# Splitting the second attention layer's score tile into two halves of heads, half a slot apart

## The chip, the cores and the metric

One Trainium2 chip, one of its cores. The metric is the device time of one launch, in microseconds (us). The work runs on five engines that each take their own instructions in order and meet at semaphores: TensorE (PE in the profile, with its weight loads as PEld), VectorE (DVE), ScalarE (ACT), GpSimd (POOL) and SyncE (SP, which here only issues transfers).

## The reference, cut to what matters

Two gated layers over 64 sequences of 128 tokens with 256 features. Each layer is cross attention with 16 heads of 16 features, then a feed-forward part (a mixture of 64 experts in layer 0, a quantised one in layer 1).

```python
x = x + jnp.tanh(g_xattn[0]) * _L0_xattn_ref(_layernorm(x), ctx_1024, ctx_1024, ...)
x = x + jnp.tanh(g_ffn[0]) * _L0_ffn_ref(_layernorm(x), ...)
x = x + jnp.tanh(g_xattn[1]) * _L1_xattn_ref(_layernorm(x), ctx_1024, ctx_1024, mask_1x1xSxS2_ik0, ...)
x = x + jnp.tanh(g_ffn[1]) * _L1_ffn_ref(_layernorm(x), ...)
# _L1_xattn_ref, per sequence and head:
scores = jnp.einsum('bhqd,bhkd->bhqk', query, key_h) * scale
scores = jnp.where(mask == 0, jnp.float32(-1000000000.0), scores)
attn = jax.nn.softmax(scores, axis=-1)
x = jnp.einsum('bhqk,bhkd->bhqd', attn, value)
```

The change touches only the third line, the attention of layer 1.

## The kernel before

The attention of a layer is a software pipeline. One sequence is a tile; a slot handles up to eight tiles at different ages at once. In the code `f`, `m`, `k`, `o`, `w`, `v`, `u` are the tiles that are 0, 1, 2, 3, 4, 5 and 6 slots old, `g` is the next one. Each engine has a written-out order of steps for a slot (`body` in `attention_pe`, `attention_act`, `attention_dve`), and a loop repeats it over the slots. Nothing is planned at run time: an engine that waits holds up all that stands behind the wait.

The score tile `tiles` is four PSUM banks wide: 16 heads of 128 by 128 scores, float32, 2048 columns on 128 partitions. A layer-1 tile uses it twice:

- `scores(m)` (L442): TensorE writes the mask bias into all four banks (`masks(0)`, L426, 16 matmuls of 32x32 in bf16), then adds query times key. The 16 features of a head lie in one of four groups of 32 rows of the array, so that matmuls of four row groups can run side by side.
- `maximum(m)` (L940): VectorE takes the row maxima of all four banks into `mt`. `maxima_t` (L473) transposes `mt`, and `shifted(m)` (L952) adds the maxima to the queries, giving `qm`.
- `scores_t(k)` (L459): one slot later, the mask bias again and then the transposed scores, shifted by the maxima, in the same four banks; `exponent(k)` (L699): ScalarE takes the exponential of all four banks into `pt`.
- `values(o)` (L487, 32-column blocks of the array), `copy_ov` (L781), `heads_to_tokens` (L568), `head_sums` and `head_norm` (L1044, L1053), `tokens_to_heads` (L578), `copy_at` (L790), `output(w)` (L557), `residual(w)` (L964), `second_stats(w)` (L972) finish a tile. `project_qk(f)` (L527) and `transposes(g)` (L507) begin one.

There is one set of four banks, so scores and transposed scores take turns in it. `mask_keys(f)` (L734) on ScalarE makes the two masked copies of the keys from the block that SyncE has loaded (`load_keys_values`, L1225 and L1227). GpSimd does `inverse_roots` (L2091), `experts_sum` (L2118) and `add_bias` (L2102) for a slot. The order on TensorE in a slot of layer 1 is:

```python
scores(m); values(o); project_qk(f); transposes(g); scores_t(k)
heads_to_tokens(o); output(w); tokens_to_heads(o); maxima_t(m)
```

Layer 0 runs the same helpers with other masks and another order; in it TensorE goes from block to block without a wait.

## Time and profile before

| | |
|---|---|
| median of 3 runs | 1837.52 us (1836.88 to 1838.45) |
| the profiled execution | 1842.04 us, its span 1840.3 us |
| busy over the span | PE 1720.2 us (93%), DVE 1382.6 (75%), ACT 1169.1 (64%), POOL 668.5 (36%) |
| granted TensorE clock, mean | 0.983 |
| chain that ended last | PE 72%, DVE 17%, ACT 8% |
| largest single lines of that chain | DVE `mt` L940 8%, PE `tiles` L459 8%, PE `tiles` L442 8%, PE `bank` L527 7%, ACT `pt` L699 6% |

The busy share is an average over four stages. Layer 1's attention lies between about 1135 and 1630 us of the span. In a timeline row the first number is the start and the second the time that the group covers; ends of matmuls are modelled, so that differences of starts are the safer reading.

### The profile page before, as it was taken

How to read it: one execution, taken by the hardware profiler on the slowest of the kernel's cores; microseconds unless marked ns; L12 is line 12 of the kernel's file. 1: busy time of each engine (PE TensorE's matmuls, PEld its weight loads, DVE VectorE, ACT ScalarE, POOL GpSimd, SP SyncE). 2: the span in 40 equal slices, each digit the busy share in tenths (PEclk: the TensorE clock that was granted, in tenths of full speed). 3: DMA queues.
4: the chain of work that ended last, by engine and by line, in shares of the span. 5: the costliest groups of instructions: out<-in, count | busy, mean ns of one | idle time of the engine just before them, and what ended most of it. 6: DMA issues, size and time to landing. Idle time of an engine off the chain costs nothing.

```text
span 1840.3 us, 54611 instructions
## 1 busy us (share of the span) xinstructions
PE 1720.2 (93%) x20134; PEld 1343.9 (73%) x20144; DVE 1382.6 (75%) x4582; ACT 1169.1 (64%) x2411; POOL 668.5 (36%) x750
## 2 busy tenths in 40 slices
PE   5999999999999799999999998999999999968845
PEld 4888888888887688888888886677777777733334
DVE  4899999999998546655555544788888888759988
ACT  3777777777777233333323334788888888858875
POOL 1111111111111147777777774222222222211157
PEclk9999999999999899999999998999999999989989
DMA  3233333333334569888988885233332333203274
GB/s 104 83 95 95 95 98 107 98 96 101 98 95 153 173 187 233 220 223 206 223 216 217 216 178 154 83 96 93 89 88 88 89 94 95 69 35 138 103 279 178
DMA packets 231350, 247.64 MB, mean 135 GB/s; under 512 B 29680, under 2 KB 207216, under 8 KB 228912
## 3 DMA queue, kind: packets, MB, share of 16 engines
q1 hardware_dynamic: 206272, 205.54, 34.8%
q0 software_dynamic: 24816, 38.62, 11.6%
q8 instruction: 163, 2.67, 0.6%
q14 instruction: 99, 0.81, 0.1%
HBM read 142.40 MB, written 101.66 MB: 133 GB/s over the span
## 4 chain that ended last, share of the span: by engine, by line
PE 72%; DVE 17%; ACT 8%; issue 1%; SPq 1%; POOL 0%; DMA 0%; POOLq 0%; DVEq 0%; ACTq 0%
DVE mt L940 8%; PE tiles L459 8%; PE tiles L442 8%; PE bank L527 7%; ACT pt L699 6%; PE bank L403 6%; PE tiles L1464 6%; PE bank L383 6%; PE bank L487 4%; PE bank L557 3%; PE tiles L426 3%; PE bank L1478 3%; PE bank L540 3%; PE bank L413 3%; DVE hmax L1852 3%; PE tiles L1446 2%
## 5 line engine op out<-in xcount | busy, mean ns | idle before, releaser
L2091 POOL TENSOR_TENSOR rstd<-var,minus_half 128x2 f32<-128x2 f32 x140 | 97.9, 700 | 650.8 <-DVE var L1020 634.8
L940 DVE TENSOR_REDUCE mt<-tiles 128x16 f32<-128x2048 f32 x128 | 293.5, 2293 | 54.2 <-PE tiles L442 54.1
L699 ACT ACTIVATE pt<-tiles 128x2048 f32<-128x2048 f32 x128 | 240.7, 1880 | 48.1 <-PE tiles L459 48.1
L1639 POOL DMA_INDIRECT accumulator<-ye,tid x128 | 208.5, 1629 | 84.6 <-DVE ye L1583 54.3
L1583 DVE TENSOR_SCALAR ye<-bank,xr 128x256 f32<-128x256 f32 x128 | 56.1, 480 | 154.6 <-PE bank L1478 154.6
L2102 POOL TENSOR_TENSOR res<-res,bias 128x256 f32<-128x256 f32 x128 | 92.9, 725 | 205.8 <-ACT xn L758 203.1
L1624 POOL DMA_INDIRECT xr<-token_rows,tid x128 | 136.9, 1070 | 72.6 <-issue 35.1
L527 PE MATMUL bank<-xt,w_q 128*128 128x128 f32 x1024 | 155.2, 285 | 1.4 <-ACT xt L707 1.4
L459 PE MATMUL tiles<-qm,qkp 32*128 32x128 f32 x4096 | 151.1, 284 | 2.6 <-DVE mt L940 2.6
L442 PE MATMUL tiles<-qkp 32*128 32x256 f32 x2048 | 151.2, 409 | 1.8 <-ACT qkp L721 1.6
L459 PEld LDWEIGHTS tiles<-qm,qkp 32*128 32x128 f32 x4096 | 126.7, 187 | 28.4 <-issue 24.5
L527 PEld LDWEIGHTS bank<-xt,w_q 128*128 128x128 f32 x1024 | 131.9, 195 | 15.6 <-issue 13.6
L487 PE MATMUL bank<-pt,vx 128*32 128x128 f32 x4096 | 140.1, 278 | 1.6 <-ACT at L790 1.0
L487 PEld LDWEIGHTS bank<-pt,vx 128*32 128x32 f32 x4096 | 105.2, 110 | 44.5 <-issue 41.1
L557 PE MATMUL bank<-w_o,at 128*128 128x256 f32 x512 | 133.1, 383 | 1.7 <-ACT at L790 1.7
L952 DVE SCALAR_TENSOR_TENSOR qm<-bank,keep,qkp 128x256 f32<-128x256 f32 x256 | 111.1, 476 | 15.7 <-PE bank L473 15.6
L442 PEld LDWEIGHTS tiles<-qkp 32*128 32x128 f32 x2048 | 87.8, 186 | 40.8 <-issue 27.5
L719 ACT ACTIVATE qkp<-bank,qb 128x128 f32<-128x128 f32 x256 | 88.7, 372 | 36.3 <-PE bank L527 36.2
L675 ACT ACTIVATE res<-bank 128x256 f32<-128x256 f32 x64 | 24.5, 383 | 135.5 <-PE bank L403 135.5
L721 ACT ACTIVATE qkp<-bank,kb,keep 128x128 f32<-128x128 f32 x256 | 106.1, 483 | 0.0
L734 ACT ACTIVATE qkp<-cxax,kb,keep 128x128 f32<-128x128 f32 x256 | 105.4, 485 | 0.0
L557 PEld LDWEIGHTS bank<-w_o,at 128*128 128x128 f32 x512 | 88.0, 192 | 9.5 <-ACT at L790 2.9
(247 smaller groups left out, 4079.9 us busy)
## 6 DMA issues: line engine op xcount, KB each, us to landing
keys_values<-res SPq DMA_DIRECT2D x64, 256.0 KB, 2.9
cxax<-keys_values SPq DMA_DIRECT2D x128, 128.0 KB, 2.5
cxax<-accumulator SPq DMA_DIRECT2D x128, 128.0 KB, 2.2
hidden_away<-h_ring SPq DMA_DIRECT2D x8, 1536.0 KB, 5.0
token_rows<-pay SPq DMA_DIRECT2D x64, 160.0 KB, 1.8
pt<-in_expert_up SPq DMA_DIRECT2D x36, 256.0 KB, 3.5
cxax<-in_ctx SPq DMA_DIRECT2D x64, 128.0 KB, 2.2
res<-in_x SPq DMA_DIRECT2D x64, 128.0 KB, 2.3
```

Source lines behind the costliest of these rows:

```text
L383: last = nc.tensor.matmul(kv_bank(n)[:, k * D:(k + 1) * D], weights_, moving, start=(c == 0), stop=(c == KC - 1))
L403: last = nc.tensor.matmul(shared_bank(n)[:, m * FS + j * P:m * FS + (j + 1) * P], w[:, c, j * P:(j + 1) * P], sxt[n % SHARED_IN][:, c, :], ...
L442: last = nc.tensor.matmul(both, qt[r % 2][rows, j, :], kp[r][rows, :, j, :], start=(L == 0), stop=True, skip_group_check=(L == 1))
L459: last = nc.tensor.matmul(tiles[:, i, n * P:(n + 1) * P], kp[r][rows, e, j, :], qm[rows, e, j, :], start=(L == 0), stop=True, skip_group_c ...
L487: last = nc.tensor.matmul(bank[7][32 * h:32 * h + 32, g * P:(g + 1) * P], vx[r][:, GH * g + h, :], pt[p][:, i, n * P:(n + 1) * P], start=T ...
L527: last = nc.tensor.matmul(o_, w[:, c, j * P:(j + 1) * P], (cx[r] if n else xt[p])[:, c, :], start=(c == 0), stop=(c == KC - 1))
L557: last = nc.tensor.matmul(bank[6][:, 0:D], at[r % 2][:, c, :], w_o[:, c, :], start=(c == 0), stop=(c == KC - 1))
L699: nc.scalar.activation(pt[r % 2][:, :, :], tiles[:, :, :], ACT.Exp).then_inc(sem("exp_done"), 1)
L940: nc.vector.tensor_reduce(mt[:, :].rearrange("p (i n c) -> p i n c", i=RT, n=2 * KC)[:, :, :, 0], tiles[:, :, :].rearrange("p i (n k) -> p ...
L952: last = nc.vector.scalar_tensor_tensor(qm[:, e, :, :], bank[4][:, MAXC[L]:MAXC[L] + P].unsqueeze(1).broadcast_to([P, KC, P]), keep[:, 1 - ...
L1624: nc.gpsimd.indirect_dma_start(out=xr[n % ROWS_IN][:, h, :], out_offset=None, in_=rows[:, :], in_offset=bass.IndirectOffsetOnAxis(ap=tid[n ...
L1639: nc.gpsimd.indirect_dma_start(out=acc[p][:, :], out_offset=bass.IndirectOffsetOnAxis(ap=tid[b % 8][:, h:h + 1], axis=0), in_=ye[r][:, h, ...
```

## The change

Layer 1's tile is cut into halves `h` = 0 and 1: half `h` holds eight heads in the banks 2h and 2h+1. A slot has two half steps. The first takes scores of half 0 of tile `m` beside transposed scores of half 1 of tile `o`; the second takes scores of half 1 of `m` beside transposed scores of half 0 of `k`. Each half step has two parts (`u`), in which the scores use two of the four row groups and the transposed scores the other two, and a piece of other work between them. `values`, `maximum` and `exponent` are halved too. `tokens_to_heads` and the steps after it move one slot later. The masked keys are made by GpSimd. The diff's core (semaphore `tg_done` and `sig_done` become `gates_out`, layer 0's helpers lose their layer-1 branches, both left out):

```diff
+        qm_ring = [qm, w_k[:, :, :].rearrange("p c d -> p (c d)").rearrange("p (e c t) -> p e c t", e=2, c=KC)]
...
+            def mask_half(h, n):
+                for i in (2 * h, 2 * h + 1):
+                    rows = slice(32 * i, 32 * i + 32)
+                    for j in range(RT):
+                        nc.tensor.matmul(tiles[32 * j:32 * j + 32, i, :], identb[rows, rows],
+                                         mask_bias[rows, n, j, :].unsqueeze(1).broadcast_to([32, 2 * KC, S]), start=True, stop=True)
+            def half_step(h, m, k, between):
+                if m is not None:
+                    b, r = m
+                    wait(pe, "exp_done", NB + 2 * (b - 2) + h + 1 if b >= 2 else 0)
+                    mask_half(h, 0)
+                    pe.wait_ge(sem("qk_out_1"), 2 * b + h + 1)
+                    pe.wait_ge(sem("keys_masked"), b + 1)
+                if k is not None:
+                    bt, rt = k
+                    ht_ = 1 - h
+                    pe.wait_ge(sem("max_done"), NB + min(2 * (bt + 1) + ht_ + 1, 2 * NB))
+                    mask_half(ht_, 1)
+                    pe.wait_ge(sem("qm_done"), NB + bt + 1)
+                for u in range(2):
+                    if u == 1:
+                        between()
+                        if m is not None:
                            pe.wait_ge(sem("s_done"), NB + 4 * b + 2 * h + 1)
                        if k is not None:
                            pe.wait_ge(sem("st_done"), NB + 4 * bt + 2 * ht_ + 1)
+                    for e in range(2):
+                        for a_ in range(2):
+                            if m is not None:
+                                i = 2 * a_ + u
+                                rows = slice(32 * i, 32 * i + 32)
+                                n = 2 * u + e
+                                s_last = nc.tensor.matmul(tiles[:, 2 * h + a_, n * P:(n + 1) * P], qt[r % 2][rows, h, :], kp[r][rows, e, h, :],
+                                                          start=False, stop=True, skip_group_check=True)
+                        for a_ in range(2):
+                            if k is not None:
+                                i = 2 * a_ + 1 - u
+                                rows = slice(32 * i, 32 * i + 32)
+                                n = 2 * (1 - u) + e
+                                t_last = nc.tensor.matmul(tiles[:, 2 * ht_ + a_, n * P:(n + 1) * P], kp[rt][rows, e, ht_, :],
+                                                          qm_ring[bt % 2][rows, e, ht_, :], start=False, stop=True, skip_group_check=True)
+                    if m is not None:
                        s_last.then_inc(sem("s_done"), 1)
                    if k is not None:
                        t_last.then_inc(sem("st_done"), 1)
@@ TensorE, body for layer 1 @@
-                scores(m)
-                    values(o)
+                    half_step(0, m, o, lambda: tokens_to_heads(w))
                     project_qk(f)
                     transposes(g)
-                    scores_t(k)
+                    values_half(0, o)
+                    half_step(1, m, k, lambda: values_half(1, o))
+                    output(w)
                     heads_to_tokens(o)
-                    output(w)
-                    tokens_to_heads(o)
                     maxima_t(m)
@@ ScalarE @@
-                    mask_keys(f)
                     normalise_first(g)
                     normalise_second(u)
+                    copy_v(f)
+                    copy_at(w)
+                    exponent_half(1, o)
+                    copy_qk(f)
+                    copy_xt(g)
                     copy_ov(o)
-                    copy_qk(f)
-                    copy_v(f)
-                    copy_xt(g)
-                    exponent(k)
-                    copy_at(o)
+                    exponent_half(0, k)
@@ VectorE @@
-                    maximum(m)
                     first_sum(n)
+                    maximum_half(0, m)
                     first_stats(n)
+                    residual(v)
+                    second_stats(v)
                     variances(n, y)
                     norming(1)
                     token_maximum(u)
+                    maximum_half(1, m)
+                    norming(1)
                     head_sums(o)
                     head_norm(o)
-                    residual(w)
-                    second_stats(w)
                     shifted(m)
-                    norming(1)
@@ SyncE, load_keys_values @@
-            wait(sp, "qk_out_1", 2 * (b - 1))
+            wait(sp, "keys_masked", b - 1)
@@ GpSimd @@
+            def mask_keys(b):
+                pool.wait_ge(sem(f"kv_in{p}"), 16 * (b - p) + 32)
+                pool.wait_ge(sem("st_done"), NB + 4 * max(b - 3, 0))
+                for j in range(KC):
+                    for e in range(2):
+                        last = G.tensor_scalar(kp[r][:, e, j, :], kvt[p][:, j * P:(j + 1) * P], keep[:, e:e + 1], kb[:, e, j:j + 1],
+                                               ALU.mult, ALU.add)
+                last.then_inc(sem("keys_masked"), 1)
             for s in range(NB + PAIR[1]):
                 inverse_roots(pool, 1, s)
+                mask_keys(s - 1)
                 experts_sum(s + 1)
                 add_bias(pool, 1, s)
```

`values_half(hf, k)` holds half of `values`' 16 matmuls and waits for `exp_done` of that half; `exponent_half(h, k)` and `maximum_half(h, m)` work on two banks, 1024 columns.

## Rows read from the trace of the kernel before

**Rows 1.** The chain that ended last, in one slot of layer 1 (start, us, what)

```profile
1348.20 2.30 DVE mt L940
...
1350.99 1.15 PE tiles L459 x32
...
1352.16 1.89 ACT pt L699
...
1354.53 1.12 PE tiles L442 x16
```

**Rows 2.** Timeline of TensorE over one slot (start, us, line, operation, names, shapes, count)

```profile
1350.55 0.44 PE L426 MATMUL tiles<-mask_bias,identb 32*32 32x512 bf16 x16
1350.92 1.17 PE L459 MATMUL tiles<-qm,qkp 32*128 32x128 f32 x32
1352.02 0.66 PE L568 MATMUL bank<-ident,ovs 128*128 128x128 f32 x4
1352.52 1.03 PE L557 MATMUL bank<-w_o,at 128*128 128x256 f32 x4
1353.49 0.44 PE L578 MATMUL bank<-ident,on 128*128 128x128 f32 x2
1353.77 0.27 PE L473 MATMUL bank<-ident,mt 128*128 128x128 f32 x1
1354.09 0.44 PE L426 MATMUL tiles<-mask_bias,identb 32*32 32x512 bf16 x16
1354.46 1.15 PE L442 MATMUL tiles<-qkp 32*128 32x256 f32 x16
1355.54 1.08 PE L487 MATMUL bank<-pt,vx 128*32 128x128 f32 x32
1356.55 1.16 PE L527 MATMUL bank<-xt,w_q 128*128 128x128 f32 x8
1357.54 0.38 PE L507 MATMUL bank<-ident,xn 128*128 128x128 f32 x2
1358.02 0.44 PE L426 MATMUL tiles<-mask_bias,identb 32*32 32x512 bf16 x16
```

**Rows 3.** All maxima of layer 1 by the view of the tile (count, durations, starts)

```profile
L940 DVE TENSOR_REDUCE mt<-tiles x64: 2292/2293/2294, 1138.2 to 1609.6; 128x16 f32<-128x2048 f32 x64
```

**Rows 4.** Timeline of TensorE over layer 0's slot, where it has no wait

```profile
403.84 0.41 PE L507 MATMUL bank<-ident,xn 128*128 128x128 f32 x2
404.18 1.17 PE L459 MATMUL tiles<-qm,qkp 32*128 32x128 f32 x32
405.29 0.44 PE L578 MATMUL bank<-ident,on 128*128 128x128 f32 x2
...
405.67 0.61 PE L527 MATMUL bank<-xt,w_q 128*128 128x128 f32 x4
...
407.46 1.03 PE L557 MATMUL bank<-w_o,at 128*128 128x256 f32 x4
408.42 1.08 PE L487 MATMUL bank<-pt,vx 128*32 128x128 f32 x32
409.43 1.16 PE L442 MATMUL tiles<-qkp 32*128 32x256 f32 x16
410.52 0.24 PE L614 MATMUL bank<-rise,sel 128*64 128x129 bf16 x1
```

**Rows 5.** Busy time of ten slots (columns: PE, PEld, DVE, ACT, POOL, clock, DMA, GB/s)

```profile
1350.50:1425.20 74.70, 73.21 (x1330) 53.24 (x1330) 61.98 (x141) 63.68 (x131) 21.20 (x30) 1.00 0.30 91
```

**Rows 6.** Timeline of VectorE in the same slot as rows 2

```profile
1355.22 0.15 DVE L1026 SCALAR_TENSOR_TENSOR nmr<-mv,rstd 128x2 f32<-128x2 f32 x1
```

**Rows 7.** Groups by line of ACT in these ten slots (count, busy us, mean ns, idle before)

```profile
L781 ACT COPY ovs<-bank 128x512 f32<-128x512 f32 x10 | 5.6, 564 | 0.0
```

**Rows 8.** Groups by line and form of POOL over the whole span

```profile
L2118 POOL TENSOR_TENSOR cxax<-cxax 128x256 f32<-128x256 f32 x64 | 46.4, 725 | 6.5 <-DMA res<-shared_out 6.5
...
L2094 POOL TENSOR_TENSOR nmr<-minus_mean,rstd 128x2 f32<-128x2 f32 x69 | 13.4, 194 | 5.4
```

More of the change, by code:

```diff
@@ L419, in attention_pe @@
             first = L * NB
-            def masks(n):
-                for i in range(RT):
+            def mask_half(h, n):
+                for i in (2 * h, 2 * h + 1):
                     rows = slice(32 * i, 32 * i + 32)
@@ L433, in scores @@
                 b, r = m
-                wait(pe, "exp_done", first + b - 1)
-                if L == 1:
-                    masks(0)
+                wait(pe, "exp_done", b - 1)
                 for j in range(KC):
@@ L441, in scores @@
                         both = tiles[:, i, :].rearrange("p (e c t) -> p e c t", e=2, c=KC)[:, :, j, :]
-                        last = nc.tensor.matmul(both, qt[r % 2][rows, j, :], kp[r][rows, :, j, :],
-                                                start=(L == 0), stop=True, skip_group_check=(L == 1))
+                        last = nc.tensor.matmul(both, qt[r % 2][rows, j, :], kp[r][rows, :, j, :], start=True, stop=True)
                 last.then_inc(sem("s_done"), 1)
@@ L450, in scores_t @@
                 b, r = k
-                pe.wait_ge(sem("max_done"), first + ahead(b, 2))
-                if L == 1:
-                    masks(1)
-                pe.wait_ge(sem("qm_done"), first + b + 1)
+                pe.wait_ge(sem("max_done"), ahead(b, 2))
+                pe.wait_ge(sem("qm_done"), b + 1)
                 for j in range(KC):
@@ L459, in scores_t @@
                             last = nc.tensor.matmul(tiles[:, i, n * P:(n + 1) * P], kp[r][rows, e, j, :], qm[rows, e, j, :],
[L460 removed]
+                                                    start=True, stop=True)
                 last.then_inc(sem("st_done"), 1)
@@ L489, in values, with values_half @@
                 last.then_inc(sem("pv_done"), 1)
+            def values_half(hf, k):
+                if k is None:
+                    return
+                b, r = k
+                pe.wait_ge(sem("exp_done"), NB + 2 * b + hf + 1)
+                pe.wait_ge(sem("v_out_1"), b + 1)
+                pe.wait_ge(sem("at_out"), NB + b)
+                for g in (2 * hf, 2 * hf + 1):
+                    for h in range(GH):
+                        n = 2 * (h // 2) + 1 - h % 2
+                        last = nc.tensor.matmul(bank[7][32 * h:32 * h + 32, g * P:(g + 1) * P], vx[r][:, GH * g + h, :],
+                                                pt[r % 2][:, g, n * P:(n + 1) * P], start=True, stop=True)
+                if hf == 1:
+                    last.then_inc(sem("pv_done"), 1)
             def transposes(f):
@@ L620, in body @@
                 g, f, m, k, o, w, v, u = (stage(lag) for lag in range(-1, 7))
-                scores(m)
                 if L == 0:
+                    scores(m)
                     if m is None:
@@ L715, in copy_qk @@
                 act.wait_ge(sem("qk_done"), first + b + 1)
-                wait(act, "st_done", first + b - 3)
+                if L == 0:
+                    wait(act, "st_done", b - 3)
                 wait(act, "qm_done", first + b - 1)
@@ L723, in copy_qk @@
                     last.then_inc(sem(sm("qk_out")), 1)
-            def mask_keys(f):
-                if f is None:
-                    return
-                b, r = f
-                p = r % 2
-                act.wait_ge(sem(f"kv_in{p}"), 16 * (b - p) + 32)
-                wait(act, "st_done", first + b - 3)
-                for j in range(KC):
-                    for e in range(2):
-                        nc.scalar.activation(kp[r][:, e, j, :], kvt[p][:, j * P:(j + 1) * P], ACT.Identity, bias=kb[:, e, j:j + 1], scale=keep[:, e:e + 1])
             def copy_v(f):
@@ L949, in shifted @@
                 dve.wait_ge(sem("mt_done"), first + b + 1)
-                wait(dve, "st_done", first + b)
+                wait(dve, "st_done", b if L == 0 else NB + 4 * max(b - 1, 0))
                 for e in range(2):
-                    last = nc.vector.scalar_tensor_tensor(qm[:, e, :, :],
+                    last = nc.vector.scalar_tensor_tensor((qm if L == 0 else qm_ring[b % 2])[:, e, :, :],
                                                           bank[4][:, MAXC[L]:MAXC[L] + P].unsqueeze(1).broadcast_to([P, KC, P]),
@@ L2058, in _ @@
             sp.wait_ge(sem("qk_out_1"), 2 * NB)
+            sp.wait_ge(sem("keys_masked"), NB)
             sp.wait_ge(sem("v_out_1"), NB)
```

39 lines of the change are left out of this document (32 added, 7 removed).

## The prediction

> **What bounds the kernel now.** I read the page first: TensorE is busy 93% of the span, yet in the chain that ended last VectorE's `mt` and ScalarE's `pt` stand among TensorE's lines. So I looked at one slot of layer 1 in the chain of waits. It is a ring through the four score banks: maxima 2.30, mask bias and transposed scores, exponential 1.89, mask bias and scores, and again maxima [rows 1]. With the two mask blocks, each 0.44 to its end (0.37 to the next block's start) [rows 2], it closes in 7.47: the slot from mask start to mask start, 1350.55 to 1358.02, is 7.47 [rows 2]. All 64 maxima are spread over 471.4 us, 63 steps of 7.48 on average [rows 3], so nearly all slots are alike.
>
> The same slot on TensorE's timeline shows how little is free there. I take differences of starts [rows 2]: mask 0.37, transposed scores 1.10, heads to tokens 0.50, output 0.97, tokens to heads 0.28, maxima transposed 0.32, mask 0.37, scores 1.08, values 1.01, projection 0.99, transposes 0.48. To see which of these hold a wait I compare with layer 0, where TensorE has none [rows 4]: output takes 0.96 there, 0.09 of it for the change to `values` behind it (its 4 passes of 256 columns are 0.87), two transposes ahead of a score block take 0.34, and the transposed maxima, one pass of 0.11, would take 0.20 with the same 0.09. Without waits the slot would be 0.37 + 1.10 + 0.50 + 0.87 + 0.28 + 0.20 + 0.37 + 1.08 + 1.01 + 0.99 + 0.34 = 7.11. **So the ring leaves TensorE only 7.47 - 7.11 = 0.36 us of idle time a slot**, and that is the most that loosening the ring can give. VectorE is busy 6.20 and ScalarE 6.37 of 7.47, GpSimd 2.12 [rows 5].
>
> **What a block on TensorE costs.** This decides the case. In layer 0 sixteen passes of 128 columns in the projection take 407.46 - 405.67 = 1.79, 0.112 each [rows 4] (a float32 matmul is recorded as two passes). The transposed scores are 32 passes on four row groups, so 8 steps, and would take 0.90; they take 1.11 (404.18 to 405.29) [rows 4] and 1.10 [rows 2]. A block of row-group matmuls thus pays 0.21 once for being entered and left. `values`, 8 steps on four column groups, takes 1.01 [rows 2, 4], 0.11 over its passes. What follows such a block pays at its own start: the projection 0.99 instead of 0.90, tokens to heads 0.28 instead of 0.22, heads to tokens 0.50 instead of 0.44 [rows 2]. These parts are paid in layer 0 too, where nothing waits, so they are not waits in disguise. The Trainium skill says the same ("TensorEngine Tiling (Array Packing)", Tiling Modes): a change of the tiling mode, as against a change of tile, drains the engine. The trace agrees, with 0.11 to 0.21 a block.
>
> **The change part by part, on TensorE.** The matmuls are the same in number of columns, and two half steps of 8 steps carry what scores (8 steps' worth) and transposed scores (8) carried. What changes is how often a mode is entered. Before, a slot has two mask blocks, two score blocks, one `values` block. After, it has two mask blocks, four score parts, two `values` blocks, and tokens to heads stands alone between two parts.
> - A score part: 4 x 0.112 + 0.21 = 0.66. Four of them, 2.64, for 1.10 + 1.08 = 2.18: +0.46.
> - Half of `values`: 4 x 0.112 + 0.11 = 0.56; two, 1.12 for 1.01: +0.11.
> - Tokens to heads between parts: 0.34 as two transposes ahead of a score block [rows 4], + 0.06 for its entry: 0.40 for 0.28: +0.12.
> - Output, now behind a score part: 0.87 + 0.06; heads to tokens no longer behind one: 0.50 - 0.06. No change. The projection follows a score part, not `values`: taken as the same.
> - Mask halves: both waits ahead of the second half are already met (below), so 16 matmuls run together as before: 0.37.
>
> In order, first half step: 0.37 + 0.66 + 0.40 + 0.66 + 0.99 + 0.34 + 0.56 = 3.98. Second: 0.37 + 0.66 + 0.56 + 0.66 + 0.93 + 0.44 + 0.20 = 3.82. **Sum 7.80 against 7.11.**
>
> **Which waits remain.** Each is walked from the end of the part that releases it.
> - Maxima of a half: VectorE takes 2.30 for 2048 columns, and 0.15 for an instruction of two columns [rows 1, 6], so (2.30 - 0.15) / 2 + 0.15 = 1.23. Half 0 is needed by the second half step's mask, after projection, transposes and `values`, 0.99 + 0.34 + 0.56 = 1.89 later: hidden with about 0.6 left. Half 1 is needed by `maxima_t`, after output and heads to tokens, 0.93 + 0.44 = 1.37 later: 1.23 plus 0.1 for the two handovers is even with it. I take 0.05 lost, bounds 0 and 0.2.
> - Exponential of a half: between 1.89 / 2 = 0.95 and 1.3; a ScalarE copy of 512 columns is 0.56 [rows 7], a straight line from it to 2048 columns' 1.89 gives 1.01. Cover 1.89 for half 1, and 0.93 + 0.44 + 0.20 = 1.57 for half 0: hidden. Without that cover a slot would pay up to 1.0.
> - The new wait inside a half step, for TensorE's own first part: a pass's row lasts 0.27 (L473) [rows 2], and 0.40 or 0.56 of other work lies between. Hidden, but in the first and last slots, where that work is missing, up to 0.3 each.
> - VectorE: one more instruction, 6.20 + 0.15 = 6.35 busy. From the end of the second half step it has half-1 maxima, head sums, head norm, `shifted` and the first sum to do before half 0 of the next slot, some 3.6 with its waits, against 0.20 + 1.37 + 0.37 + 0.66 + 0.40 + 0.66 = 3.66 on TensorE. Even, with 0.6 of cover behind it on TensorE.
> - ScalarE loses the four key copies and gains one instruction: it is below 6.37 + 0.15. It gives nothing, since it was not what the slot waited for except in the exponential.
> - GpSimd gains four instructions of 128 columns. No row shows one; nearest are 0.19 for two columns and 0.725 for 256 with two inputs [rows 8]. Between 0.19 and 0.73, I take 0.46, the middle: 1.84 a slot, 2.12 + 1.84 = 3.96 of 7.8. Behind them in its queue stand the experts' sum (one tile ahead) and the bias (needed several slots later). The keys are used two slots after they are masked. The two key loads of SyncE's queue are now released by `keys_masked` of a tile long done and by the copy of the values as before. Nothing is late up to 0.7 each.
>
> **Sum.** A slot 7.80 + 0.05 = 7.85, 0.38 more than 7.47. Of the 63 steps [rows 3] I take 60, and leave the first few, which the start of the stage sets, as they are: 60 x 0.38 = 23. Last slots, with bare half steps and output one slot later: 0, bounds 0 and 4. So 1842.0 + 23 = 1865 for an execution like the profiled one (span 1840.3, and 1.7 around it). The median of the runs lies 4.5 below that execution: **1860 us.** If the fixed parts were 0.05 smaller at each of the more boundaries, or the handovers 0.3 longer, the slot is 7.6 to 8.15, and the time 1845 to 1880.
>
> **The rivals.**
> - *The boundaries are free when row groups alternate, and the ring's slack comes out.* TensorE then runs at its 7.11, plus the 0.1 at `maxima_t`: 7.2, 0.27 less a slot, 60 x 0.27 = 16: 1821. For it: the ring really is loosened (maxima 1.23 and exponential 1.0 beside work). Against it: layer 0's blocks pay with no wait ahead [rows 4]. It decides if the four more entries and exits cost under 0.36 together, against 0.69 by the rows. 15%.
> - *Same time:* they cost about 0.36. 5%.
> - *VectorE or GpSimd holds TensorE as well.* VectorE's stretch ahead of the half-0 maxima is even with TensorE's; 0.5 us more there, through GpSimd instructions of 0.7 delaying the first sum, makes the slot 8.3: 60 x 0.8 = 48, 1886. In the slot before, GpSimd's work lies where VectorE reads PSUM, so no row shows the two in each other's way. 10%. The Trainium skill ("SBUF — State Buffer", SBUF: two separate sides) has a lock by which a GpSimd instruction and a VectorE one with two SBUF inputs exclude each other; the first sum is of that kind. By it the half-0 maxima could come one GpSimd instruction later.
> - *It doesn't do what it says:* scores and transposed scores of one part do not run side by side. Each part then has 8 steps, 4 x 0.45 = 1.8 more, 9.6 a slot, 60 x 2.1 = 126, 1964. All four row groups differ and all four banks differ, as now. 3%.
>
> **How the numbers follow.** The forecast's case has 67%, own range 1845 to 1880. Faster 15% and a little of the forecast's lower edge: 0.17. Within 0.2% (3.7 us, what a measurement of this kernel can tell from no change) 0.06. Slower 0.77. The range that should hold 8 of 10 leaves out most of the free-boundary case and the last: 1835 to 1886.
>
> **What would show it.** In the trace after: slots of 7.8 to 7.9; TensorE's score parts 0.66 from start to next start; almost no idle time on TensorE but a little ahead of `maxima_t`; the chain of layer 1 nearly all TensorE; VectorE and ScalarE with more idle time than before. Wrong if parts take 0.5, if mask halves stand apart at 0.37 each, or if slots fall under 7.47.

## The result and the profile after

The changed kernel takes 1872.65 us (median of 4 runs, 1871.31 to 1873.27), the kernel before, beside it on the same chip, 1837.99 (1836.88 to 1838.91). The ratio is 1.0181, with a 95% interval of 1.0168 to 1.0194: slower by 34.7 us. The profiled execution took 1871.31, its span 1869.6.

The chain that ended last on the page of the changed kernel, shares of the span by engine:

```profile
PE 85%; DVE 9%; ACT 2%; issue 1%; POOL 1%; DMA 1%; SPq 1%; POOLq 0%; DVEq 0%; ACTq 0%
```

Before it was PE 72%, DVE 17%, ACT 8%. In layer 1's steady slots the ring through the score banks is gone from the chain. In one slot, the counterpart of [rows 1], the chain holds nothing but TensorE's own pieces (start, us, what; the pieces between are TensorE's too):

```profile
1403.68 0.36 PE tiles L427 x16
...
1405.93 1.06 PE bank L611 x4
1406.99 0.44 PE bank L622 x4
1407.43 0.15 PE bank L511
```

Ten slots, as in [rows 5] (stretch and its length, then busy us of PE, PEld, DVE, ACT, POOL, then clock, DMA share, GB/s):

```profile
1400.00:1478.24 78.24, 78.24 (x1506) 58.27 (x1490) 62.45 (x151) 52.77 (x101) 38.51 (x71) 1.00 0.29 87
```

TensorE is recorded as busy all the time at the full granted clock, and ten slots last 78.24 where they lasted 74.70. VectorE has 6.25 a slot (6.20 before), ScalarE 5.28 (6.37), GpSimd 3.85 (2.12). So no other engine holds a steady slot any longer, though only ScalarE has less to do in it, and the slot became longer all the same.

The counterpart of [rows 2], TensorE's timeline over one slot (L427 mask, L457 scores, L464 transposed scores, L632 tokens to heads, L581 projection, L561 transposes, L540 values, L611 output, L622 heads to tokens, L511 transposed maxima):

```profile
1399.68 0.43 PE L427 MATMUL tiles<-mask_bias,identb 32*32 32x512 bf16 x16
1400.05 0.38 PE L457 MATMUL tiles<-qkp 32*128 32x128 f32 x2
...
1400.71 0.44 PE L632 MATMUL bank<-ident,on 128*128 128x128 f32 x2
1401.08 0.38 PE L457 MATMUL tiles<-qkp 32*128 32x128 f32 x2
...
1401.73 1.16 PE L581 MATMUL bank<-xt,w_q 128*128 128x128 f32 x8
1402.73 0.38 PE L561 MATMUL bank<-ident,xn 128*128 128x128 f32 x2
1403.04 0.65 PE L540 MATMUL bank<-pt,vx 128*32 128x128 f32 x16
1403.61 0.43 PE L427 MATMUL tiles<-mask_bias,identb 32*32 32x512 bf16 x16
1403.98 0.38 PE L457 MATMUL tiles<-qkp 32*128 32x128 f32 x2
...
1404.63 0.65 PE L540 MATMUL bank<-pt,vx 128*32 128x128 f32 x16
1405.21 0.38 PE L457 MATMUL tiles<-qkp 32*128 32x128 f32 x2
...
1405.86 1.13 PE L611 MATMUL bank<-w_o,at 128*128 128x256 f32 x4
1406.83 0.60 PE L622 MATMUL bank<-ident,ovs 128*128 128x128 f32 x4
1407.27 0.31 PE L511 MATMUL bank<-ident,mt 128*128 128x128 f32 x1
1407.51 0.43 PE L427 MATMUL tiles<-mask_bias,identb 32*32 32x512 bf16 x16
```

Read it by differences of starts: mask 0.37 twice, the four score parts 0.66, 0.65, 0.65 and 0.65, tokens to heads 0.37, projection 1.00, transposes 0.31, the two halves of `values` 0.57 and 0.58, output 0.97, heads to tokens 0.44, transposed maxima 0.24. They sum to 7.83.

The counterpart of [rows 3] (durations min/median/max in ns, first and last start), and then the half exponential and the key masks from the page's groups (busy us, mean ns of one):

```profile
L1004 DVE TENSOR_REDUCE mt<-tiles x128: 1214/1226/1228, 1141.7 to 1640.0; 128x8 f32<-128x1024 f32 x128
```

```profile
L762 ACT ACTIVATE pt<-tiles 128x1024 f32<-128x1024 f32 x128 | 130.9, 1023 | 31.7 <-PE tiles L464 25.6
...
L2195 POOL TENSOR_SCALAR qkp<-cxax,keep,kb 128x128 f32<-128x128 f32 x256 | 111.1, 448 | 0.0
```

**Where the time went.** I cut layer 1's attention at four marks on TensorE: the last matmul of the context's keys and values, and the transposed maxima of the 5th, the 60th and the 64th tile; its end is the first transposition of the stage behind it.

| us | before | after | difference |
|---|---|---|---|
| start, to the 5th tile | 44.2 | 50.2 | +6.0 |
| 55 steps, 5th to 60th | 410.7 (7.467 each) | 430.3 (7.824 each) | +19.6 |
| 60th to 64th | 29.9 | 30.7 | +0.8 |
| drain, after the 64th | 15.4 | 18.9 | +3.5 |
| all of it | 500.1 | 530.0 | +29.9 |

The two profiled executions differ by 1871.31 - 1842.04 = 29.3, so all of it is there. The medians differ by 34.7: the profiled execution of before, which is not among the four, lies 4.1 above their median of 1837.99, and that of after lies 1.3 below its own (29.3 + 4.1 + 1.3).

### The profile page after: what moved, and what is told of

Same layout as the page of the kernel before. It is cut to its first block, busy times and chain, and to the rows that moved or that the text cites. A ratio compares the mean times of both kernels' runs of the same rounds, so it can differ in the third digit from the quotient of the medians.

```text
span 1869.6 us, 57242 instructions
## 1 busy us (share of the span) xinstructions
PE 1758.1 (94%) x21168; PEld 1380.1 (74%) x21168; DVE 1386.8 (74%) x4646; ACT 1098.6 (59%) x2219; POOL 779.3 (42%) x1006
## 4 chain that ended last, share of the span: by engine, by line
PE 85%; DVE 9%; ACT 2%; issue 1%; POOL 1%; DMA 1%; SPq 1%; POOLq 0%; DVEq 0%; ACTq 0%
PE bank L581 10%; PE tiles L457 8%; PE bank L611 6%; PE bank L404 6%; PE tiles L1529 6%; PE bank L384 6%; PE bank L540 4%; PE tiles L496 4%; PE tiles L482 4%; PE bank L525 3%; PE bank L1543 3%; PE bank L594 3%; PE bank L414 3%; PE bank L622 3%; DVE hmax L1917 3%; PE tiles L427 3%
## 5 line engine op out<-in xcount | busy, mean ns | idle before, releaser
L1004 DVE TENSOR_REDUCE mt<-tiles 128x8 f32<-128x1024 f32 x128 | 156.9, 1226 | 85.0 <-PE tiles L457 85.0
L457 PE MATMUL tiles<-qkp 32*128 32x128 f32 x2048 | 186.7, 301 | 0.6 <-PE tiles L464 0.4
L457 PEld LDWEIGHTS tiles<-qkp 32*128 32x128 f32 x2048 | 137.2, 189 | 54.5 <-issue 51.7
L993 DVE TENSOR_REDUCE mt<-tiles 128x16 f32<-128x2048 f32 x64 | 146.8, 2293 | 30.1 <-PE tiles L482 30.0
L581 PE MATMUL bank<-xt,w_q 128*128 128x128 f32 x1024 | 157.0, 288 | 1.4 <-ACT xt L770 1.4
L762 ACT ACTIVATE pt<-tiles 128x1024 f32<-128x1024 f32 x128 | 130.9, 1023 | 31.7 <-PE tiles L464 25.6
L581 PEld LDWEIGHTS bank<-xt,w_q 128*128 128x128 f32 x1024 | 133.5, 197 | 10.0 <-ACT xt L770 2.1
L611 PE MATMUL bank<-w_o,at 128*128 128x256 f32 x512 | 138.5, 393 | 1.7 <-ACT at L843 1.7
L834 ACT COPY ovs<-bank 128x512 f32<-128x512 f32 x128 | 77.7, 607 | 100.4 <-PE bank L540 98.0
L753 ACT ACTIVATE pt<-tiles 128x2048 f32<-128x2048 f32 x64 | 120.5, 1884 | 1.2 <-PE tiles L496 1.2
L2195 POOL TENSOR_SCALAR qkp<-cxax,keep,kb 128x128 f32<-128x128 f32 x256 | 111.1, 448 | 0.0
L843 ACT COPY at<-bank 128x256 f32<-128x256 f32 x128 | 47.6, 372 | 90.9 <-PE bank L632 90.7
L611 PEld LDWEIGHTS bank<-w_o,at 128*128 128x128 f32 x512 | 87.1, 190 | 17.0 <-ACT at L843 2.7
L1016 DVE SCALAR_TENSOR_TENSOR qm<-bank,keep,qkp 128x256 f32<-128x256 f32 x192 | 83.8, 478 | 14.3 <-PE bank L511 14.2
```

The lines of the kernel that those rows point to most:

```text
L457: s_last = nc.tensor.matmul(tiles[:, 2 * h + a_, n * P:(n + 1) * P], qt[r % 2][rows, h, :], kp[r][rows, e, h, :], start=False, stop=True, ...
L581: last = nc.tensor.matmul(o_, w[:, c, j * P:(j + 1) * P], (cx[r] if n else xt[p])[:, c, :], start=(c == 0), stop=(c == KC - 1))
L611: last = nc.tensor.matmul(bank[6][:, 0:D], at[r % 2][:, c, :], w_o[:, c, :], start=(c == 0), stop=(c == KC - 1))
L753: nc.scalar.activation(pt[r % 2][:, :, :], tiles[:, :, :], ACT.Exp).then_inc(sem("exp_done"), 1)
L762: nc.scalar.activation(pt[r % 2][:, 2 * h:2 * h + 2, :], tiles[:, 2 * h:2 * h + 2, :], ACT.Exp).then_inc(sem("exp_done"), 1)
L993: nc.vector.tensor_reduce(mt[:, :].rearrange("p (i n c) -> p i n c", i=RT, n=2 * KC)[:, :, :, 0], tiles[:, :, :].rearrange("p i (n k) -> p ...
```

## The experiments

The theory: in the steady slot TensorE pays for every change between blocks, about 0.7 us a slot, of which 0.36 is left over when the waits that went away are set against it; and no other engine holds it. In experiments 3 to 9 some expectation was missed each time, which is said there. The rivals were GpSimd's masked keys, waits for maxima or exponential, and the wait of TensorE for its own first part.

**1. The move of the masked keys alone**, in the kernel before (the core of the edit; the wait for `keys_masked` on TensorE and SyncE comes with it):

```diff
@@ ScalarE, body @@
-                    mask_keys(f)
@@ GpSimd @@
             for s in range(NB + PAIR[1]):
                 inverse_roots(pool, 1, s)
+                mask_keys(s - 1)
                 experts_sum(s + 1)
```

> The kernel before with one part of the change alone: layer 1's keys are masked by GpSimd (the two semaphores of the gates become one, to make room). Theory A (ScalarE's key copies lay outside the ring): slot 7.47, within 0.2% of before. Rival D (GpSimd reading SBUF gets in VectorE's way, or ScalarE's relief helps): slot off by 0.1 or more, +-6 us.

Measured: 1839.64, ratio 0.9997 (0.9985 to 1.0009), a slot of 7.467. In the steady slot the edit costs nothing and brings nothing. The lock in the Trainium skill ("SBUF — State Buffer", SBUF: two separate sides), by which a GpSimd instruction and a VectorE one with two SBUF inputs exclude each other, is not tried there: in none of these slots does the first sum, which is of that kind, stand beside a GpSimd instruction, and it takes 0.415 as before. Where it does meet one, at the start of the layer, the traces agree with the page: the sum takes 0.93. The section after these experiments comes back to it.

**2. One change of mode more**, in the changed kernel: the transposes stand between `values` and the masks.

```diff
                     project_qk(f)
-                    transposes(g)
                     values_half(0, o)
+                    transposes(g)
                     half_step(1, m, k, lambda: values_half(1, o))
```

> The changed kernel with one order swapped on TensorE in layer 1: projection, half of values, transposes, instead of projection, transposes, half of values. The same instructions and waits, one change of block form more in a slot. Theory A (TensorE bounds the changed kernel and each entry and exit of a block form is paid): slot 7.82 + 0.09 + 0.04 = about 7.95, 60 slots x 0.13 = +8 us, 1880. Rival B (what was lost is waits between engines, block changes are free): slot 7.82, 1872 to 1873.

Measured: 1880.36, ratio 1.0221 (1.0203 to 1.0239), a slot of 7.982. The same matmuls in another order cost 0.158 a slot. By differences of starts, projection takes 1.09 instead of 1.00 (`values` behind it) and transposes 0.37 instead of 0.31 (behind `values`), and nothing else moves by more than 0.01. This is the price of a boundary by itself, with no wait added: the block form's cost is real.

**3 and 4. A quarter of the maxima's work**, in the kernel before (3) and in the changed one (4). The maxima are taken over 32 of the 128 keys only, so VectorE's instruction is short and everything else stays.

```diff
-   tiles[:, :, :].rearrange("p i (n k) -> p i n k", n=2 * KC)
+   tiles[:, :, :].rearrange("p i (n k) -> p i n k", n=2 * KC)[:, :, :, 0:32]
```

> The kernel before, with layer 1's maxima taken over the first 32 of each head's 128 keys only: the part left out is three quarters of the columns of the row maximum, so VectorE's step in the ring falls from 2.30 to about 0.68 us. Theory A (TensorE's own work without waits is 7.11 a slot, the ring left only 0.36): slot 7.1 to 7.2, about -20 us against before, 1817. Rival B (the ring is all that bounds it and TensorE's 93% is padded): slot 7.47 - 1.6 = 5.9, -95 us.

> The changed kernel with the same cut of the maxima (first 32 of 128 keys of each head; each half's maxima fall from 1.23 to about 0.4 us). Theory A (TensorE is busy all of the slot): slot 7.82 less 0.03 at the transposed maxima, time within 3 us of the changed kernel, 1870 to 1873. Rival B (VectorE or a wait for it holds TensorE): several tenths less a slot, -15 us or more.

Measured before: 1826.47, ratio 0.9925 (0.9898 to 0.9953), a slot of 7.300. Measured after: 1865.10, ratio 1.0135 (1.0117 to 1.0153), a slot of 7.787. VectorE's instruction falls from 2.29 to 0.69 in the first and from 1.23 to 0.43 in the second. Taking 1.6 us out of the ring shortens a slot of before by only 0.17, all of it between transposes and mask (0.48 to 0.31), since TensorE is next; the 7.1 to 7.2 expected were missed by 0.1. In the changed kernel the slot gives back 0.04, all of it at `maxima_t` (0.24 to 0.20), which is the whole wait for the maxima there. Its median came out 5 under the range expected, which is not explained. Two waits are left in before's slot, on TensorE's timeline (`maxima_t` to mask 0.33, not 0.20; output to tokens to heads 0.97, not 0.87). The view of waits puts TensorE's weight loads in these two places down to ScalarE's exponential (7.9 us in 27 slots) and to VectorE's head norm (9.3 in 27):

```profile
1405.40 1.03 PE L557 MATMUL bank<-w_o,at 128*128 128x256 f32 x4
1406.37 0.44 PE L578 MATMUL bank<-ident,on 128*128 128x128 f32 x2
1406.65 0.27 PE L473 MATMUL bank<-ident,mt 128*128 128x128 f32 x1
1406.98 0.44 PE L426 MATMUL tiles<-mask_bias,identb 32*32 32x512 bf16 x16
```

Without them the slot would be 7.30 - 0.13 - 0.10 = 7.07, next to the 7.11 that the prediction summed. The changed kernel's slot without its wait is 7.79, so the finer blocks cost 0.72 by the traces, where the prediction had 0.69.

**5. The two parts of a half step together**, with the work between them put behind them. It leaves two score blocks in a slot where there were four.

```diff
-                    half_step(0, m, o, lambda: tokens_to_heads(w))
+                    half_step(0, m, o, lambda: None)
+                    tokens_to_heads(w)
...
-                    half_step(1, m, k, lambda: values_half(1, o))
+                    half_step(1, m, k, lambda: None)
+                    values_half(1, o)
```

> The changed kernel with nothing between the two parts of a half step: tokens to heads goes behind the first half step, the second half of values behind the second. Two block changes fewer inside each half step, but TensorE now waits for its own first part. Theory A (a part's last pass lasts 0.27 and its handover 0.05, so the wait costs about 0.2 and a fresh weight load 0.1, as much as the two changes): slot 7.8 to 7.9, within 4 us of 1872. Rival C (the work between the parts is what makes the scheme pay, as it hides a long wait): slot 8.2 or more, +20 us.

Measured: 1903.89, ratio 1.0393 (1.0312 to 1.0474), a slot of 8.34. One of the four executions took 1928.47, which raises the ratio; by the medians it is 1.034. A miss of my theory by half a microsecond a slot; the rival was right. TensorE's timeline inside the half step:

```profile
1400.61 0.28 PE L457 MATMUL tiles<-qkp 32*128 32x128 f32 x2
1400.62 0.28 PE L464 MATMUL tiles<-w_k,qkp 32*128 32x128 f32 x2
1401.10 0.38 PE L457 MATMUL tiles<-qkp 32*128 32x128 f32 x2 [0.20 <-PE tiles L464]
```

From the last pass of part one to the first of part two it is 0.48 where two passes in a row are 0.11 apart: the pass itself lasts 0.28, and 0.20 more go by before TensorE passes its own semaphore. That is 0.37 lost per half step, and the first half step's mask takes 0.46 now, not 0.37. The wait that the prediction called hidden is hidden only by the piece of work between the parts; with that cover gone the slot pays 0.52, the changes saved already taken off.

**6. `values` whole again**, both halves inside the second half step.

```diff
-                    values_half(0, o)
-                    half_step(1, m, k, lambda: values_half(1, o))
+                    if o is not None:
+                        pe.wait_ge(sem("exp_done"), NB + 2 * o[0] + 1)
+                    half_step(1, m, k, lambda: (values_half(0, o), values_half(1, o)))
```

> The changed kernel with both halves of values in the second half step, between its parts: one block of values in a slot instead of two, so one entry and exit fewer, but less work covers the half-0 maxima (1.30 instead of 1.87). Theory A: slot 7.82 - 0.2 for the entry and exit + 0.1 for the maxima that now come late = 7.7 to 7.78, 1866 to 1870. Rival B (block changes are free): slot 7.9, 1877.

Measured: 1872.91, ratio 1.0182 (1.0158 to 1.0206), slots of 7.83 to 7.86: no gain, a miss. The block was saved and a wait came for it:

```profile
1403.70 0.38 PE L561 MATMUL bank<-ident,xn 128*128 128x128 f32 x2
1404.03 0.55 PE L427 MATMUL tiles<-mask_bias,identb 32*32 32x512 bf16 x16
1404.51 0.38 PE L457 MATMUL tiles<-qkp 32*128 32x128 f32 x2
```

The mask takes 0.48 to the next start, not 0.37, because the maxima of half 0 and the exponential have lost `values`' 0.57 of cover. In this slot the exponential ends at 1403.89, and the first eight mask matmuls start at 1404.03; the maxima end at 1404.03, and the other eight start at 1404.18. The piece that looked like pure cost was also cover.

**7. The masked keys back on ScalarE**, in the changed kernel (GpSimd's `mask_keys(s - 1)` removed, `mask_keys(f)` in ScalarE's body before `normalise_first(g)`).

> The changed kernel with one part undone: the keys are masked by ScalarE at the head of its slot, as before. Theory A (GpSimd's part only keeps ScalarE in time): ScalarE's exponential of half 1 comes about 0.9 later, against 0.75 of cover: slot 7.9 to 8.0, +5 to +12 us. Rival D (the GpSimd work is itself part of the loss): slot below 7.82, faster than the changed kernel.

Measured: 1870.01, ratio 1.0158 (1.0135 to 1.0180), a slot of 7.823. A miss: I had expected ScalarE to be late. It has an idle stretch of 1.35 in each slot even so. With experiment 1 this settles that the move to GpSimd has no part in the steady slot, in either direction. In the start of the layer it has one, as the chain shows there: with the keys on ScalarE the first transposed maxima come 13.8 behind the first mark instead of 14.7, of which 0.4 is left at the fifth tile (start 49.8, not 50.2).

**8. The changed kernel once more, and its first scores whole.** Two runs about the start of the layer. In the second the first tile's scores are made in one step of four row groups, not in two half steps of two.

```diff
-                    half_step(0, m, o, lambda: tokens_to_heads(w))
+                    bare = m is not None and m[0] == 0
+                    if bare:
+                        first_scores(m)
+                    else:
+                        half_step(0, m, o, lambda: tokens_to_heads(w))
...
-                    half_step(1, m, k, lambda: values_half(1, o))
+                    if not bare:
+                        half_step(1, m, k, lambda: values_half(1, o))
```

> The changed kernel itself once more, beside the kernel before on the same chip, as the control of the others. Theory A: slot 7.82, 1.0181 of before as first measured, 1871 to 1875. If the first profile's start (50.2 us) was an accident of the granted clock, it is 44 to 47 here.

> The changed kernel, but tile 0, which has no partner in its half steps, takes its scores on all four row groups at once, in two parts instead of four. Theory F (part of what the change costs at the start of layer 1, 6 us from the last key/value matmul to the fifth tile's transposed maxima, is that a half step without a partner uses half the row groups, twice 2.5 us at the lower clock for 2.0 before): start 2 to 3 us shorter, slot unchanged at 7.82, 1870. Rival G (the start is set by the norms and loads of the first tiles, not by TensorE): start unchanged at 50.

Measured: again 1870.23, ratio 1.0173 (1.0154 to 1.0192), start 50.1; first scores whole 1872.49, ratio 1.0183 (1.0164 to 1.0201), start 50.3. The theory that the first tile's half steps alone make the start longer falls: TensorE was done sooner and then stood 4.53 for VectorE's maxima, and the first transposed maxima came 14.68 behind the first mark in both runs.

**9. VectorE's order in the start.** First the maxima of half 0 ahead of the first sum, then also `nmr` ahead of the maxima of half 1.

```diff
-                    first_sum(n)
                     maximum_half(0, m)
+                    first_sum(n)
...
                     token_maximum(u)
+                    norming(1)
                     maximum_half(1, m)
-                    norming(1)
```

> The changed kernel with one pair exchanged in VectorE's order for layer 1: the maxima of half 0 come before the first sum, as the whole maxima did before the change. The question is the start of layer 1, from the last matmul of the keys and values of the context to the transposed maxima of the fifth tile: 44.2 us in the kernel before, 50.2 in the changed one. Theory G (VectorE's order): in the start the first sum waits for GpSimd (0.65 to 2.3 us a slot), and the maxima queue behind it; with the maxima first a part of this is hidden, the start is 47 to 49 and the time 1868 to 1870. Theory H (the start is long because the half-step scores themselves are slow and each tile needs two of them in turn): start 50, time as the changed kernel's, 1870 to 1873. In the steady slot both expect 7.82, since TensorE has no idle time to give; if VectorE's first sum is then late for the next tile's chain it could rise to 7.9.

> As the run before it, and the second part of the norm for the next tile (the instruction nmr, 0.16 us) is put ahead of the maxima of half 1 as well, so that ScalarE's normalised tile doesn't wait for these maxima. Theory G: the start falls to 44 to 47 us and the time to 1865 to 1868, with a slot of 7.82 to 7.87, since nmr's 0.16 us stands ahead of the maxima of half 1, for which the transposed maxima already wait. Theory H: start 50, and 60 times up to 0.1 more in the slot, 1872 to 1878.

Measured: the first exchange 1871.78, ratio 1.0163 (1.0134 to 1.0192), start 50.0, slot 7.824; both 1882.54, ratio 1.0227 (1.0202 to 1.0253), start 52.3, slot 8.01. This theory falls too: the first exchange brings the first transposed maxima only from 14.7 to 14.4 behind the first mark. The second run, whose slot rose by 0.18 where 0.1 was the most expected, shows how tight VectorE's path to `maxima_t` is. Its timeline in that run:

```profile
1405.57 0.16 DVE L1090 SCALAR_TENSOR_TENSOR nmr<-mv,rstd 128x2 f32<-128x2 f32 x1 [0.49 <-POOL rstd L2157]
1405.65 1.23 DVE L1004 TENSOR_REDUCE mt<-tiles 128x8 f32<-128x1024 f32 x1
```

and TensorE's (heads to tokens to transposed maxima 0.60, not 0.44):

```profile
1406.33 0.60 PE L622 MATMUL bank<-ident,ovs 128*128 128x128 f32 x4
1406.93 0.33 PE L511 MATMUL bank<-ident,mt 128*128 128x128 f32 x1
```

Here TensorE waits 0.16, and yet the row of the ten slots from 1400 to 1480 has it busy 80.00 of 80.00. A busy share of 100% does not say that there is no wait: it says that none is longer than what the modelled ends cover. Only differences of starts showed it.

**10. Maxima without the mask**, in the kernel before. The maxima need not know the mask: any shift of a row gives the same quotient, and the unmasked maximum is never below the masked one, so nothing overflows. What is given up is range: where a masked key's score lies far above all others of its row, their exponentials can run out of float32 at the small end. So the bias matmuls of the scores go, and a small VectorE instruction restores the shift of rows whose keys are all masked.

```diff
-                if L == 1:
-                    masks(0)
...
-                        last = nc.tensor.matmul(both, qt[...], kp[...], start=(L == 0), stop=True, skip_group_check=(L == 1))
+                        last = nc.tensor.matmul(both, qt[...], kp[...], start=True, stop=True)
...
+                nc.vector.tensor_scalar(heads, heads, shut[:, 0:1], None, ALU.add).then_inc(sem("shut_done"), 1)
```

> A way to loosen the ring without more block changes: the kernel before, where the mask bias is left out of the scores from which the maxima are taken (softmax keeps its value under any shift of a row), and a row whose keys are all masked gets the bias by a small VectorE instruction on the 16 maxima, outside the ring. One mask block of two is gone. Theory A: ring 7.47 - 0.37 = 7.10, TensorE 7.11 - 0.37 = 6.74: slot 7.1, 63 x 0.37 = -23 us, 1815. Rival E (VectorE's extra instruction or the order of its slot takes the place): slot 7.3, -10 us.

Measured: 1815.21, ratio 0.9866 (0.9843 to 0.9888), a slot of 7.100, and layer 1's attention 474.4 instead of 500.1. It is faster than both kernels. On TensorE's timeline the mask of the scores is gone, and the rest is as in [rows 2]:

```profile
1402.52 0.44 PE L427 MATMUL tiles<-mask_bias,identb 32*32 32x512 bf16 x16
...
1405.73 0.27 PE L473 MATMUL bank<-ident,mt 128*128 128x128 f32 x1
1406.06 1.15 PE L441 MATMUL tiles<-qkp 32*128 32x256 f32 x16
```

The slot fell by 7.467 - 7.100 = 0.367, a mask block's 0.37 [rows 2]: the block stood both in the ring and in TensorE's own work, so taking it out shortens both.

## Why the prediction was right, point by point

The forecast was 1860 with a range of 1835 to 1886, slower at 0.77; 1872.65 is in it. The mechanism of the steady slot was right, and its term nearly so; but 20.4 of the 34.7 us come from it, and the rest from two terms taken as nothing and from an offset that did not hold. All of these fell the same way, and together they used up half of the range's upper side.

- *TensorE has only 0.36 us of slack in a slot.* Right: with a quarter of the maxima's work, before's slot went down by 0.17 and kept 0.23 in two other waits.
- *A slot of 7.85.* Measured 7.824. The score part was put at 0.66 and took 0.65 to 0.66, half of `values` 0.56 and took 0.57 to 0.58, tokens to heads 0.40 and took 0.37, mask 0.37 and took 0.37. Output was put at 0.93 and took 0.97: the price of leaving a score part, put at 0.06, is 0.10 to 0.11 (the projection takes 1.00 behind a part and 0.89 behind tokens to heads in experiment 5). It was made up for by tokens to heads and by the transposes, put at 0.34 and measured 0.31.
- *Maxima of a half 1.23, exponential 1.01, GpSimd's instruction 0.46.* Measured 1.226, 1.023 and 0.448. The wait at `maxima_t` was put at 0.05 and is 0.04.
- *The wait for TensorE's own first part is hidden.* Right as the kernel stands, shown by experiment 5. The prediction counted only the pass's 0.27 against it; it is 0.48, of which 0.20 is the handover. The 0.37 between the parts (tokens to heads) only just covers what exceeds the usual 0.11.
- *VectorE is even with TensorE ahead of half 0's maxima.* It had 0.36 to spare there, the idle time ahead of half 0's maxima on its timeline in the changed kernel:

```profile
1401.84 1.23 DVE L1004 TENSOR_REDUCE mt<-tiles 128x8 f32<-128x1024 f32 x1 [0.36 <-PE tiles L457]
```

  So the rival in which VectorE or GpSimd holds TensorE did not come in the steady slot; in the first slots it did (next point). The second run of experiment 9 shows the same engine costing 0.18 a slot as soon as one wait of 0.49 is put ahead of the maxima of half 1.
- *The start is taken as unchanged, 0.* **This is the term that was mis-sized: it is +6.0.** The prediction's 60 slots left out the first few "as they are", without walking through them. Of the 6.0, 3.5 have come by the first transposed maxima (14.7 behind the first mark, before 11.2), 1.8 come in the step to the second (9.25, before 7.43), -0.1 and twice 0.36 in the three after that. TensorE's timeline in the changed kernel shows what the first tile meets:

```profile
1134.72 0.63 PE L427 MATMUL tiles<-mask_bias,identb 32*32 32x512 bf16 x8
1135.28 2.52 PE L457 MATMUL tiles<-qkp 32*128 32x128 f32 x16
1137.72 2.08 PE L581 MATMUL bank<-xt,w_q 128*128 128x128 f32 x8
...
1140.71 2.52 PE L457 MATMUL tiles<-qkp 32*128 32x128 f32 x16
1144.88 0.48 PE L511 MATMUL bank<-ident,mt 128*128 128x128 f32 x1 [1.66 <-DVE mt L1004]
```

  and the same in the kernel before:

```profile
1135.45 0.65 PE L426 MATMUL tiles<-mask_bias,identb 32*32 32x512 bf16 x16
1136.03 2.09 PE L442 MATMUL tiles<-qkp 32*128 32x256 f32 x16
...
1141.50 0.45 PE L473 MATMUL bank<-ident,mt 128*128 128x128 f32 x1 [0.94 <-ACT xt L707]
```

  While no older tile fills the other two row groups, a half step keeps only half of the array's rows at work: 2.44 to the next start for half a tile, where the whole tile took 2.02, both at a granted clock of 0.50. From the first mask to the first transposed maxima it is 10.2 against 6.1. But TensorE waits 1.66 at the end of it, and the chain to that point does not run through the half steps. It runs through GpSimd and VectorE (start, us, what; the same pieces of one slot earlier, from 1133.22 on, are left out):

```profile
1138.35 0.89 POOL qkp L2195 x3
...
1139.63 0.44 POOL qkp L2195
1140.08 0.70 POOL cxax L2184
...
1141.65 1.21 DVE mt L1004
...
1143.60 1.24 DVE mt L1004
```

  The masked keys, 1.74 a slot from first to last, stand in it twice, ahead of the experts' sum for which VectorE's first sum waits. The prediction held that with instructions of up to 0.7 each nothing would be late; that is so in the steady slot, and not at the start. And here GpSimd and VectorE do get in each other's way: GpSimd's bias addition starts 0.07 before VectorE's first sum, and the sum takes 0.93, where its median over the layer is 0.416:

```profile
1140.73 0.72 POOL L2168 TENSOR_TENSOR res<-res,bias 128x256 f32<-128x256 f32 x1
1140.80 0.93 DVE L1045 TENSOR_TENSOR res<-res,cxax 128x256 f32<-128x256 f32 x1 [2.26 <-POOL cxax L2184]
```

  It happens three times in full in the first slots, and three times in experiment 1's as well, where the maxima stand ahead of the first sum and the start was 41.5. In five other runs with the same chain (the changed kernel's repetition, experiments 2, 5 and 6, and the whole first scores) the first transposed maxima lie 14.68 to 14.70 behind the first mark, though the granted clock from 1130 to 1142 goes from 0.59 to 0.97 among them. With a quarter of the maxima (experiment 4) it is 13.1, less by the 1.6 taken from the two maxima. So neither TensorE nor its clock sets this point. TensorE's own path is nearly as long: with the keys back on ScalarE (experiment 7) or the maxima ahead of the first sum (first run of 9) the chain runs through the two half steps, and the point lies at 13.8 and 14.4. In the step to the second tile the chain is TensorE's, with its half steps, and then 1.24 of maxima of half 1, at a lower clock than in before's start (columns as in the ten slots' row, the changed kernel first):

```profile
1142.00:1160.00 18.00, 14.56 (x150) 10.74 (x150) 11.06 (x22) 5.03 (x11) 7.83 (x15) 0.59 0.34 103
```

```profile
1142.00:1160.00 18.00, 15.39 (x236) 10.59 (x226) 9.77 (x19) 10.36 (x21) 5.46 (x8) 0.73 0.30 92
```

  What the runs do not settle is what the start would be with both paths short: whole first scores (experiment 8), the keys on ScalarE (7) and VectorE's order (9) were each tried alone, and each left it at 50, because the other path came next. How the 5.3 of the first tile and the step behind it divide between half steps, GpSimd's masks and the lower clock is therefore argued from the chains, not shown by a run.
- *Last slots 0, bounds 0 and 4.* The drain took 3.5 more and the steps before it 0.8: the upper bound, not the value, was near. The reason given there, output a slot later and bare half steps, fits: from the 64th transposed maxima to the last output block it is 13.5 (1641.34 to 1654.88) against 9.8 (1615.12 to 1624.92). What would be saved without them was not tried.
- *The profiled execution lies 4.5 over the median, and so will the next.* This offset did not carry over. Before's executions spread from 1836.3 to 1844.5 (17 beside experiment 1), and its traced one lay near the upper end. Experiment 1, with the same slot, had a start of 41.5 us at a granted clock of 0.98 (1130 to 1142) and 0.92 (1142 to 1160), where the traced one had 44.2 at 0.69 and 0.73; if the clock is the reason, which one trace of each does not show, 2.7 of the 4.5 lie there. In the changed kernel and its variants the start was 49.8 to 52.3 every time, at 0.50 to 0.69 from 1142 to 1160.

The sum, from the forecast to the result: 23 for the slots came out as 20.4 for the 59 steps from the fifth tile on, the start gives +6.0, the drain +3.5, the rest of the program -0.6; that is 29.3 instead of 23, +6.3. The offset of 4.5 that was not there and the 1.3 from the traced execution to its median make 1860.5 + 6.3 + 4.5 + 1.3 = 1872.6. That the forecast lay 12 low and still inside its range owes something to the range's width, not to the working of the start and the end.

The rival with free boundaries (1821) is refuted by experiment 2. The rival in which scores and transposed scores do not run side by side is refuted by the parts' 0.65 to 0.66 from start to next start, where it would need 1.1.

## What to carry to other kernels

Before a ring of waits is loosened, sum the engine that is next without its waits: here 0.36 of a slot's 7.47 was all there was to win, and the finer interleaving cost 0.7 in block boundaries. Walk through the first and the last slots by themselves: a step that is full only with two tiles of different ages in it runs half empty there, twice, and work that was moved to an engine with time to spare (here the masked keys on GpSimd) can stand in the first tile's chain though no steady slot waits for it. Look first for work that lies both in the ring and on the next engine; a mask block that the maxima do not need was worth 1.3%, more than any reordering.

## What the runs showed of the hardware that was not expected

- A TensorE instruction that waits for TensorE's own last matmul starts 0.48 us after that one's start: 0.28 of the pass and 0.20 more. VectorE starts 0.05 after the end of such a pass (1401.79 to 1401.84 in the changed kernel).
- One change between block forms more costs TensorE 0.16 a slot with no wait anywhere near it (experiment 2), with the same number of matmuls issued.
- GpSimd's multiply-and-add of 128 x 128 float32 by two per-partition scalars takes 0.448. It slowed nothing in VectorE's steady slot (ratio 0.9997), where no VectorE instruction with two SBUF inputs stood beside it.
- Where such an instruction starts just after one of GpSimd's, it is held up: VectorE's sum of 128 x 256 took 0.93 instead of 0.416 with GpSimd's bias addition started 0.07 before it (changed kernel, 1140.80), and its `nmr` of two columns 0.68 instead of 0.15 with GpSimd's experts' sum started 0.06 before it (kernel before, 1133.39).
- The granted clock from 1142 to 1160, in the first slots of the layer, was 0.73 in the kernel before, 0.92 in experiment 1 and 0.50 to 0.69 in every trace of the changed kernel and its variants, between levels of 1.2 and 2.4 GHz. In two of these (experiments 4 and 6) it had been 0.98 and 0.97 from 1130 to 1142 and was 0.50 from 1142 to 1151; TensorE had been idle 4.6 and 4.5 of the 12 us before.
